# Wide attention: causal mask added by VectorE, scores and turned probabilities in separate banks, scores two steps ahead

## The reference, cut to what matters

```python
q = xn @ w_q.T; k = ctx @ w_k.T; v = ctx @ w_v.T        # 32 x 128 x 1024, 16 heads of 64
scores = q_h @ k_h.T / sqrt(64)                          # 32 x 16 x 128 x 128
scores = where(causal, scores, -inf)                     # causal = tril(ones)
probs  = softmax(scores, axis=-1)
x = x + tanh(g) * ((probs @ v_h) merged @ w_o.T)
```

## Time and profile before

| | |
|---|---|
| median of 3 runs | 1741.85 us (1741.49 to 1743.46) |
| the profiled execution's own time | 1740.41 us |
| its span | 1738.7 us |
| mean granted clock of TensorE | 0.961 of full speed |
| busy share over the whole span | TensorE 91%, VectorE 62%, ScalarE 54%, GpSimd 33% |
| the stage of the change | scores from about 316 to 741 us of the span |

### The profile page before, as it was taken

The page is one execution under the profiler, slowest core; times in us unless marked ns, Lnnn a source line. Parts: engine busy times, 40 slices in busy tenths (PEclk is TensorE's granted clock), DMA queues, the critical chain, the costliest instruction groups (busy, mean ns, idle before and its releaser), DMA issues. The chain is left out here.

```text
span 1738.7 us, 46429 instructions
## 1 busy us (share of the span) xinstructions
PE 1579.3 (91%) x17384; PEld 1056.4 (61%) x17384; DVE 1074.8 (62%) x2332; ACT 932.9 (54%) x2341; POOL 570.3 (33%) x1033
## 2 busy tenths in 40 slices
PE   3998899999999999987987799979999988998898
PEld 2555454677777777765765456647777764555354
DVE  5687777566666666655166788962332235778676
ACT  3877535555556555534444466534344336776354
POOL 3565238232323323210121345300000005664672
PEclk8999899999999999989999799979999998999899
DMA  8544220000000000010103334110000016552000
GB/s 188 140 132 126 81 70 7 7 5 8 5 8 8 5 8 5 2 49 12 37 1 91 108 106 115 35 38 0 1 0 0 0 37 156 141 143 63 7 19 25
DMA packets 114001, 86.40 MB, mean 50 GB/s; under 512 B 19344, under 2 KB 110736, under 8 KB 113808
## 3 DMA queue, kind: packets, MB, share of 16 engines
q1 hardware_dynamic: 106592, 81.30, 17.1%
q10 hardware_dynamic: 7216, 2.45, 0.9%
HBM read 22.88 MB, written 2.10 MB: 14 GB/s over the span
## 5 line engine op out<-in xcount | busy, mean ns | idle before, releaser
L1105 DVE TENSOR_REDUCE neg_max<-scores 128x8 f32<-128x1024 f32 x192 | 226.7, 1181 | 69.9 <-PE scores L723 26.1
L2201 POOL TENSOR_TENSOR probs<-probs,inverse 128x512 f32<-128x512 f32 x128 | 133.3, 1041 | 314.5 <-DVE inverse L2406 314.5
L2340 ACT ACTIVATE probs<-scores,neg_max 128x128 f32<-128x128 f32 x512 | 180.7, 387 | 5.3 <-DVE neg_max L2398 5.3
L969 ACT ACTIVATE probs<-turned 128x1024 bf16<-128x1024 f32 (+1 forms) x128 | 131.1, 1024 | 84.8 <-PE turned L746 84.8
L1859 ACT ACTIVATE hidden_f<-hb_f,b_f 128x512 f32<-128x512 f32 x128 | 87.9, 687 | 128.9 <-PE hb_f L1805 128.7
L554 POOL TENSOR_TENSOR k_all<-k_all,k_parts 128x512 f32<-128x512 f32 x24 | 27.7, 1156 | 324.1 <-ACT k_parts L895 324.1
L1814 PEld LDWEIGHTS yb_f<-w_f,hidden_f 128*128 128x128 f32 x1024 | 119.2, 192 | 14.8 <-issue 14.8
L2331 ACT ACTIVATE heads_t<-heads 128x512 f32<-128x512 f32 x64 | 38.2, 597 | 166.4 <-PE heads L2266 166.4
L1814 PE MATMUL yb_f<-w_f,hidden_f 128*128 128x128 f32 x1024 | 119.3, 275 | 0.0
L1805 PE MATMUL hb_f<-xn_all_f,w_f 128*128 (+1 forms) x256 | 116.8, 600 | 0.0
L2340 ACT ACTIVATION_READ_ACCUMULATOR probs<-scores,neg_max 128x1 f32 x512 | 116.8, 228 | 0.0
(11 more groups left out here) (343 smaller groups left out, 3767.9 us busy)
## 6 DMA issues: line engine op xcount, KB each, us to landing
k_rep<-k_parts SPq DMA_DIRECT2D x144, 128.0 KB, 2.5
q_rep<-q_parts SPq DMA_DIRECT2D x129, 128.0 KB, 2.5
dense<-both SPq DMA_DIRECT2D x120, 64.0 KB, 2.1
ctx_t<-in_ctx_t_dram SPq DMA_DIRECT2D x24, 256.0 KB, 4.0
conv_weights_or_copies<-k_parts SPq DMA_DIRECT2D x32, 128.0 KB, 2.7
conv_weights_or_copies<-q_parts SPq DMA_DIRECT2D x32, 128.0 KB, 2.5
w_f<-in_L_ffn_W_dram SPq DMA_DIRECT2D x16, 256.0 KB, 3.1
x_state<-in_x_dram SPq DMA_DIRECT2D x4, 512.0 KB, 7.6
```

Of the source, the lines that this page charges most:

```text
L969: nc.scalar.activation(probs[:, b % 2, pair, :], turned[:, :], ACT.Exp, **bias).then_inc(s["exp_done"], 1)
L1105: v.tensor_reduce(neg_max[:, b % 2, 8 * pair + first:8 * pair + 8], scores[pair][:, first * S:].rearrange("p (h k) -> p h k", k=S), axis=X ...
L2201: nc.gpsimd.tensor_tensor(p4, p4, inverse[:, n % 2, CH * h:CH * h + CH].unsqueeze(2).to_broadcast([P, CH, S]), ALU.mult).then_inc(s["prob_ ...
L2340: last = nc.scalar.activation(probs[:, n % 2, h, c * S:(c + 1) * S], scores[n % 2][:, i * S:(i + 1) * S], ACT.Exp, bias=neg_max[:, n % 2, ...
```

## The change

The mask is no longer written by matmuls. `causal` and `causal_swapped` (bf16) go, and a table `future` (fp32, 0 where a key may be seen, +1e30 where not) comes. q is copied with the factor -scale, so that the score banks hold the negated scores. In `maximum` the single reduction is replaced by 8 instructions `tensor_tensor_reduce`, one for each head: 128 scores from PSUM plus the table, written to a new SBUF tile `masked`, and the minimum of the row (which is the negated maximum) into `neg_max`. ScalarE takes its exponentials from `masked` with scale -1. It may begin with the first half when that half is done.

PSUM is divided anew: two banks `scores` and two banks `turned` in place of two sets of two banks that served both. So `score(n)` now waits for `maximum(n-1)`, and `turn(n)` also for the copies of turn(n-1). The scores, and the fills with them, run one iteration further ahead: score(n+2) stands where score(n+1) stood, the loop begins one iteration earlier. On VectorE the two copies of turn(n) now stand ahead of maximum(n+2).

```diff
         def fills(n):
-            group, part = divmod(n + 4, 4)
+            group, part = divmod(n + 5, 4)
...
             def score(n):
...
-                wait(pe, s["pt_done"], 2 * n - 2)
-                for h, table in enumerate((st.causal, st.causal_swapped)):
-                    for r in range(2):
-                        nc.tensor.matmul(scores[n % 2][rows((r + h) % 2), h * 512:h * 512 + 512], st.identb[rows(r), rows(r)],
-                                         table[rows(r), :].unsqueeze(1).to_broadcast([DKW, CH, S]), start=True, stop=False,
-                                         skip_group_check=True)
+                wait(pe, s["max_done"], 2 * n)
                 for c in range(CH):
                     for h in range(2):
-                        last = nc.tensor.matmul(scores[n % 2][:, h * 512 + c * S:h * 512 + (c + 1) * S],
+                        last = nc.tensor.matmul(scores[:, h * 512 + c * S:h * 512 + (c + 1) * S],
...
-                                                start=False, stop=(c == CH - 1), skip_group_check=True)
+                                                start=(c == 0), stop=(c == CH - 1), skip_group_check=True)
...
             def turn(n):
                 pe.wait_ge(s["exp_done"], 2 * n + 2)
+                wait(pe, s["pt_done"], 2 * n)
...
-                            last = nc.tensor.transpose(scores[n % 2][:, at:at + DKW], probs[rows(r), n % 2, h, c * S:(c + 1) * S],
+                            last = nc.tensor.transpose(turned[:, at:at + DKW], probs[rows(r), n % 2, h, c * S:(c + 1) * S],
...
-            for n in range(-4, NO + 1):
+            for n in range(-5, NO + 1):
...
-                score(n + 1)
+                score(n + 2)
                 turn(n)
                 contexts(n - 1)
...
             def exponents(n, h):
-                act.wait_ge(s["max_done"], n + 1)
+                act.wait_ge(s["max_done"], 2 * n + h + 1)
...
-                                                scores[n % 2][:, i * S:(i + 1) * S], ACT.Exp,
+                                                masked[:, n % 2, i * S:(i + 1) * S], ACT.Exp, scale=-1.0,
...
             def maximum(n):
...
-                v.tensor_reduce(neg_max[:, n % 2, :], scores[n % 2][:, :].rearrange("p (h k) -> p h k", k=S),
-                                axis=X_AXIS, op=ALU.max, negate=True).then_inc(s["max_done"], 1)
+                for h in range(2):
+                    for i in range(CH * h, CH * h + CH):
+                        own = slice(i * S, (i + 1) * S)
+                        last = v.tensor_tensor_reduce(out=masked[:, n % 2, own], in0=scores[:, own], in1=st.future[:, :], scale=1.0,
+                                                      scalar=3.0e38, op0=ALU.add, op1=ALU.min, accum_out=neg_max[:, n % 2, i:i + 1])
+                    last.then_inc(s["max_done"], 1)
...
-                if n % 4 == 3:
-                    normalise((n + 5) // 4)
-                maximum(n + 1)
+                if n % 4 == 2:
+                    normalise((n + 6) // 4)
                 copy_turned(n, 0)
                 copy_turned(n, 1)
+                maximum(n + 2)
                 for f in todo[2:]:
                     keep(f)
                 invert(n + 1, 0)
```

More of the change, by code:

```diff
@@ L210, in setup @@
         x_in, g_in, zeroed, consts = [sem(f"x_in{c}") for c in range(4)], sem("g_in"), sem("zeroed"), sem("consts")
-        w_zero, swapped = sem("w_zero"), sem("swapped")
+        w_zero, padded = sem("w_zero"), sem("padded")
         block = ctx.enter_context(nc.Block())
@@ L230, in _ @@
             nc.gpsimd.memset(st.row0[:, :], 1.0)
-            nc.gpsimd.memset(st.causal[:, :], 0.0)
-            nc.gpsimd.memset(st.causal_swapped[:, :], 0.0)
+            nc.gpsimd.memset(st.future[:, :], 0.0)
             nc.gpsimd.memset(st.own_rows[:, :, :], 0.0)
@@ L245, in _ @@
                                     base=0, pattern=[[0, P]], channel_multiplier=-1)
-            nc.gpsimd.affine_select(out=st.causal[:, :], in_=st.causal[:, :], compare_op=ALU.is_ge, fill=NEVER,
+            nc.gpsimd.affine_select(out=st.future[:, :], in_=st.future[:, :], compare_op=ALU.is_ge, fill=-NEVER,
                                     base=0, pattern=[[-1, P]], channel_multiplier=1).then_inc(consts, 1)
@@ L253, in _ @@
             nc.gpsimd.memset(st.spread[:, :, :], 0.0)
[L254 to L262, removed]
+            nc.gpsimd.memset(st.ones_b[:, :], 1.0).then_inc(padded, 1)
+            pool.wait_ge(padded, 1)
+            nc.gpsimd.memset(heads_apart(st.v_pad, 0, 1), 1.0)
+            nc.gpsimd.memset(heads_apart(st.v_pad, 1, 1), 1.0)
         @block.scalar
@@ L2143, in attention_wide @@
         heads_t = sb("heads_t", [P, 2, CH * S])
-        scores = [ps("scores0", 2 * CH * S), ps("scores1", 2 * CH * S)]
+        masked = sb("masked", [P, 2, 2 * CH * S])
+        scores, turned = ps("scores", 2 * CH * S), ps("turned", 2 * CH * S)
         made = [ps("made0", 512), ps("made1", 512)]
@@ L2322, in keep @@
                     last = nc.scalar.activation(q_t[:, group % 2, 2 * part:2 * part + 2, :].rearrange("p c q -> p (c q)"),
-                                                made[f % 2][:, :], ACT.Copy, scale=scale)
+                                                made[f % 2][:, :], ACT.Copy, scale=-scale)
                 last.then_inc(s["act_kept"], 1)
@@ L2390, in copy_turned @@
                 wait(dve, s["pv_done"], n - 1)
-                v.tensor_copy(probs_t[:, n % 2, h, :], scores[n % 2][:, h * 512:h * 512 + 512]).then_inc(s["pt_done"], 1)
+                v.tensor_copy(probs_t[:, n % 2, h, :], turned[:, h * 512:h * 512 + 512]).then_inc(s["pt_done"], 1)
             def maximum(n):
@@ L2419, in _ @@
             normalise(0)
-            for n in range(-4, NO + 2):
+            for n in range(-5, NO + 2):
                 todo = fills(n)
@@ L2585, in program @@
         st.ones, st.tri = sb("ones", [P, P]), sb("tri", [P, P])
-        st.row0, st.causal, st.causal_swapped = (sb(n, [P, P], BF16) for n in ("row0", "causal", "causal_swapped"))
+        st.row0, st.future = sb("row0", [P, P], BF16), sb("future", [P, P])
         st.ident32 = sb("ident32", [P, 32])
```

## The result

The changed kernel takes 1754.4 us (median of 7 runs, 1748.6 to 1760.9) beside 1741.9 us for the kernel before (7 runs, 1739.2 to 1748.1, in the same comparison). The ratio is 1.0074, with a 95% interval of 1.0055 to 1.0093: slower by 0.7%. The profiled execution's span is 1750.4 us against 1738.7.

A forecast was written before the change was run, and what follows sets the result against it. It took two of four steps as bound by the ScalarE, VectorE, GpSimd loop and two by TensorE. Cycles 20.3, last steps -1.3 and 0.3, head 5 made 24.3 us on 1740.4, hence 1765; range 1738 to 1792.

The forecast's parts named there:

- 20.3 us for the cycles: Attention steps: 15 cycles of four steps, each 1.35 us longer (28.58 against 27.23).
- the head: Stage start: the fills and a score of one quarter 0 step move ahead of the first context product, costing 5 us.
- its own signs of being wrong: Eight under 1.75 us, first inverse still waiting for ScalarE, or context products under 27.2 us for four.
- What binds before: Kernel before: two of four steps hang on the ScalarE, VectorE, GpSimd loop, two on TensorE; dropping mask matmuls gives 26.59.
- The price of the eight: VectorE's mask instructions: 0.285 us each, 2.28 us for eight, bounds 1.60 and 2.74.
- the read of the row's result: VectorE: reading out each mask instruction's row minimum adds 0.083 us, taken from ScalarE's rows.
- turning point of 1.75 us: VectorE's eight: below 1.75 us (0.22 each) the change is faster; chance 0.13 faster, 0.07 a tie about it.
- the 1755 us it worked out: VectorE's eight by the skill's figures: 2.07 us without the read, making the sum end near 1755 us.
- I take 0: ScalarE's exponentials from SBUF: 0 to 0.03 us more each, taken as 0 since in a run they overlap.
- if VectorE proved fast: ScalarE's exponentials from SBUF: with a fast VectorE their cover is gone and 0.24 us counts in each step.
- VectorE's queue formula: Context product to the next through VectorE's queue: 6.41 us plus 0.61 for each k copy of fills standing behind.
- the rival's lower clock: TensorE: a tenth of the steps at the lower clock, about 6 us more each, 1800 us; chance 0.04.

The follow-up runs named there:

- e4: The kernel before with its four mask matmuls per step left out and nothing in their place: 1734.3 us, ratio 0.9946.
- e6: e5 with the masked scores written back in place into PSUM and the exponentials reading them there: 1741.6 us, ratio 0.9977 to the kernel before.
- e5: The kernel before with VectorE's eight mask instructions into SBUF replacing mask matmuls and reduction; banks, score distance and order kept: 1749.0 us, ratio 1.0029.
- e1: The changed kernel with VectorE's eight mask instructions put back ahead of the two turned copies: 1756.4 us, ratio 1.0066 to the kernel before.
- e2: The changed kernel with ScalarE's context copy moved behind the first half of the exponentials: 1733.1 us, ratio 0.9933 to the kernel before.
- e7: e2 with VectorE reordered: maximum, first inverse, turned copies, fills' copies, second inverse: 1717.3 us, ratio 0.9844 to the kernel before.
- e8: e7 with VectorE's two turned copies moved behind the copies of the fills: 1713.7 us, ratio 0.9828 to the kernel before.

## Why the prediction came out as it did

**The direction and the range held, for a reason other than the one given.** The forecast was 1765, the time 1754; slower was right. Its sum had 20.3 us for the cycles, and they cost 4.1 (15 times 0.27). That the time still came out 12.5 us above the kernel before is in part luck: the head cost 4.4 as foreseen, but 2.9 us lie ahead of the stage and 1.1 in the lower clock of the last steps, and its sum had neither. Of its own signs of being wrong the first came true: the eight took under 1.75 us.

**What binds before: right.** e4 shows it: without the mask the cycle is 26.56, against 26.59 in the prediction's sum.

**The price of the eight: the term that was mis-sized.** It was taken at 2.28 and measured 1.68. The plain sum's 0.20 was the right neighbour (0.21), but the read of the row's result was added at 0.083 by ScalarE's rows, and on VectorE it runs beside the next instruction (83 ns long, 0.01 at most in the distance, by the plain sum's estimated 0.20; no run leaves the read out). By the prediction's own turning point of 1.75 us that would have been a tie or faster. The 2.07 us for eight that the prediction set beside its sum are above the measured 1.68 too, so that the 1755 us it worked out from them is near to 1754 by chance. The Trainium skill has the nearer figure in its Vector Engine (DVE) Microarchitecture Reference, section 5.2: for built-in operations one column a cycle and about 75 ns an instruction, hence 208 ns as an estimate for 128 columns. The trace agrees with 0.21 where the result goes to SBUF; with the result in PSUM (e6) it shows 0.25.

**"I take 0" for the exponentials from SBUF: the step that failed.** The prediction argued that in a run the longer latency would overlap. It does not: 0.042 us more from one to the next, in the changed kernel and in e5, and gone in e6. The rows of copies (628 and 597 ns) bounded it at 0.03 and were too low. The rule of the Trainium skill that it cited (VectorE: DVE Perf Modes, "The TRN2 errata"), 224 fixed cycles from SBUF against 172 from PSUM, is 43 ns, and the trace agrees: 0.042. The prediction did write that this cost would count in each step if VectorE proved fast; that is what came. The two errors were of opposite sign, and that they left the time within the range is luck. With 1.68 and 0 its formula gives 6.42, 7.15, 6.80, 6.42, a cycle of 26.79 and with the head a tie; with 1.68 and seven times 0.042 the loop is at 6.61 and 7.09, measured 6.59 and 7.07.

**VectorE's queue formula: right within 0.11 us, but binding in one step alone.** C + 3.61 for the first inverse is 0.11 + 1.20 + 1.68 + 0.61 = 3.60. With eleven instructions, where it binds, it gives 7.05, 7.05, 7.77 and 7.07 (the fourth is ScalarE's), and the trace shows 7.01, 7.08, 7.88, 7.07. At the real price it would ask for 6.42, and ScalarE's loop asks for 6.59 first. Only the step from 0 to 1 was VectorE's: the formula gives 7.14, the trace 7.25. In both kernels it is 0.11 short there: from k3's start to the inverse behind its copy it took 1.67, and in the changed kernel it was 1.78 (518.17 to 519.95).

**What costs nothing: right for the banks and the waits** (e5 and e1: no step changes). **Head: right**, 5 taken, 4.4 measured. **The clock**: it stayed at 1.00 through the steady part, so the rival's lower clock in a tenth of the steps didn't come. It did fall to 0.50, the lower level of 1.2 GHz, for the last two steps, after a stretch in which TensorE was busy for only part of the time (no fills are left there): from 752 to 769 us, and in the kernel before from 748 to 755. Half a turn then shows 0.69 us in place of 0.47 and the contexts 1.97 in place of 1.09. The two steps are 6.8 and 7.7 long where the ones before them are 6.6: 1.35 more, against 0.22 in the kernel before. This 1.1 us is most of the 1.6 of the 63 steps that the cycles don't explain.

**What the prediction did not see** is that the change had already laid the ground for a gain. Scores two steps ahead free the exponentials from the contexts of the step before, but ScalarE's queue still held the context copy in front of them. e2 shows it: one line of ScalarE's loop moved, 1.13 us a cycle. What the same move gives without the second step ahead, no run shows.

## What to carry to other kernels

When work is run one step further ahead to break a chain, look at every in-order queue that the chain passes: the data may be early while the instruction still stands behind one that waits. Here the second step ahead was worth nothing until ScalarE's queue was turned (e2). Another order on VectorE was worth 0.1 us a cycle before that (e1) and 0.6 after (e7 against e2, where the inverses were moved too). An engine that is busy for 99% may still not set the step; cutting out its work alone, as e4 does, tells it in one run.

## What the runs showed of the hardware that was not expected

- The same exponential of 128 columns with a row sum costs 0.385 us from start to start out of SBUF (e5) and 0.343 out of PSUM (e6), though each reads its row sum out in between. The mean length of a record, 390 and 387 ns, doesn't show it.
- Reading out the row result: 0.083 us more for each instruction on ScalarE, by an estimate from two different runs of instructions in the prediction's rows, and nothing that shows on VectorE, where the 83 ns record starts together with the next instruction.
- VectorE's mask instruction is 0.21 us apart with its result in SBUF (e5) and 0.25 with it in PSUM (e6).
- Executions of one kernel differ by half a percent: the kernel before took 1739.4 to 1749.0 us over 21 runs on one chip, with mean granted clocks of 0.954 to 0.960. In the profiles the stage's own start moved between 302.0 us (e5, and before 302.1) and 309.6 us (e6), though no stage ahead of it was changed. With medians alone, differences of 4 us, as e7 to e8, can't be told; the lengths of the steps, which repeat to 0.01 us, tell them.
